# Two heads of each group of four take their second-layer mask as a factor applied by GpSimd, and all rounds run in one piece

## The reference

```
scores = einsum('bhqd,bhkd->bhqk', q, k) / sqrt(DK)
scores = where(mask[:, None, :, :] == 0, NEG, scores)      # NEG = -65504, mask is [16, 256, 1601]
attn = softmax(scores, axis=-1)
out = einsum('bhqk,bhkd->bhqd', attn, v)
```

## Time and profile before

| | |
|---|---|
| median of 3 runs | 5445.89 us (5444.5 to 5447.28) |
| profiled execution | 5421.1 us, of it the span of the core 5419.8 us |
| PE busy | 4887.3 us (90%) |
| DVE busy | 3598.6 us (66%) |
| ACT busy | 2794.9 us (52%) |
| POOL busy | 641.3 us (12%) |
| mean granted PE clock | 0.933 |

### The profile page before, as it was taken

How to read it: one execution, slowest core, us unless ns; L and a number is a source line. 1 busy time by engine, 2 the same in 40 slices (tenths; PEclk the granted TensorE clock), 3 DMA queues, 4 the chain that set the end, 5 groups by cost and what they waited for, 6 DMA issues and landing times.

```text
span 5419.8 us, 103495 instructions
## 1 busy us (share of the span) xinstructions
PE 4887.3 (90%) x41312; PEld 2745.4 (51%) x41312; DVE 3598.6 (66%) x8383; ACT 2794.9 (52%) x5505; POOL 641.3 (12%) x660
## 2 busy tenths in 40 slices
PE   5888888888888888889899999999999999999999
PEld 2455555555555555554455544554455444554456
DVE  4666666666666666566667777777777777777774
ACT  1565565656555556665454444444445444444454
POOL 1111111110111111011110101101010101001000
PEclk7799898989999999897899999999999999999999
DMA  2112222222212222222222222222222222222222
GB/s 60 34 45 52 44 46 52 58 54 50 53 45 43 48 58 54 58 49 70 59 72 69 77 65 70 76 69 65 70 72 69 75 61 78 74 70 64 73 49 65
DMA packets 167992, 327.09 MB, mean 60 GB/s; under 512 B 25656, under 2 KB 76624, under 8 KB 167520
## 3 DMA queue, kind: packets, MB, share of 16 engines
q1 hardware_dynamic: 167520, 320.49, 24.3%
HBM read 237.40 MB, written 4.19 MB: 45 GB/s over the span
## 4 chain that ended last, share of the span: by engine, by line
PE 39%; DVE 8%; SPq 2%; POOL 1%; issue 1%; DMA 1%; ACT 1%; DVEq 0%
PE sums L695 7%; PE a L658 7%; PE d L771 6%; PE a L759 5%; PE a L666 4%; DVE d L811 3%; SPq L1072 2%; PE d L679 1%; PE d L601 1%; PE d L581 1%; PE d L733 1%; PE a L608 1%; PE a L641 1%; DMA kc<-k_hi 1%; PE d L614 1%
## 5 line engine op out<-in xcount | busy, mean ns | idle before, releaser
L967 ACT ACTIVATE probs_c<-a 128x512 f32<-128x512 f32 (+1 forms) x3584 | 1833.9, 563 | 1994.5 <-PE a L666 1992.7
L811 DVE CUSTOM_DVE_ANT_0 d<-d,mcross_q 128x404 f32<-128x404 f32 x2048 | 1138.0, 606 | 341.6 <-PE d L679 337.6
L803 DVE TENSOR_REDUCE chunk_max<-d 128x2 f32<-128x808 f32 x1024 | 1003.2, 998 | 289.0 <-PE d L679 280.5
L695 PE MATMUL sums<-probs_c,vc 128*32 128x256 f32 x13312 | 1119.9, 410 | 13.4 <-PEq L1234 13.2
L666 PE MATMUL a<-qc,kc 25*128 25x256 f32 (+1 forms) x6656 | 931.1, 341 | 129.7 <-ACT probs_c L967 98.5
L666 PEld LDWEIGHTS a<-qc,kc 25*128 25x128 f32 (+1 forms) x6656 | 543.0, 187 | 825.9 <-issue 393.3
L679 PE MATMUL d<-kc,qc 24*128 24x404 f32 x4096 | 912.4, 458 | 47.0 <-DVE chunk_max L811 12.9
L771 PE MATMUL d<-w_back,hidden 128*128 128x128 f32 x4352 | 558.4, 283 | 28.8 <-DVE chunk_max L811 28.8
L759 PE MATMUL a<-xT_e,w_in 128*128 128x256 f32 x2176 | 576.5, 412 | 0.0
L771 PEld LDWEIGHTS d<-w_back,hidden 128*128 128x128 f32 x4352 | 533.5, 197 | 66.8 <-DVE chunk_max L811 39.5
L658 PE MATMUL a<-mcross_k,ident_b 128*128 128x512 bf16 (+1 forms) x1792 | 547.4, 379 | 12.4 <-ACT probs_c L967 12.2
(11 more groups left out here) (157 smaller groups left out, 4441.6 us busy)
## 6 DMA issues: line engine op xcount, KB each, us to landing
w_in<-in_experts SPq DMA_DIRECT2D x272, 256.0 KB, 3.1
w_back<-in_experts SPq DMA_DIRECT2D x272, 256.0 KB, 2.9
kc<-k_hi SPq DMA_DIRECT2D x1024, 50.0 KB
ctxT<-in_ctxT SPq DMA_DIRECT2D x32, 800.5 KB, 5.2
kc<-k_lo SPq DMA_DIRECT2D x512, 50.0 KB
mask_words<-in_mcross SPq DMA_DIRECT2D x32, 800.5 KB
mask_words<-in_mcrossT SPq DMA_DIRECT2D x32, 768.0 KB
out_x<-xe SPq DMA_DIRECT2D x32, 128.0 KB, 1.8
```

What stands on the lines that cost most here:

```text
L695: last = pe.matmul(acc[HP * j:HP * j + HP, :], T["vc"][x.p][0:x.kn, v0:v0 + HP], probs_of(T, x)[0:x.kn, j, half:half + S], start=x.j == 0, ...
L803: done = dve.tensor_reduce(T["chunk_max"][:, x.g % 2, x.i, x.j:x.j + 2, x.c], tile[:].rearrange("p (h n) -> p h n", h=2)[:, :, 0:CHUNK], A ...
L811: done = dve.tensor_tensor_reduce(some, some, mask, 1.0, -3e38, ALU.add, ALU.max, T["chunk_max"][:, x.g % 2, x.i, x.j + h, x.c:x.c + 1])
L967: act.activation(probs_of(T, x)[0:x.kn, x.j, 0:n], tile[0:x.kn, 0:n], ACT.Exp, scale=SCALE).then_inc(M["a_read"], 1)
```

## The change

For heads 0 and 1 of each group (`j < BY_POOL`, the first beat of every kp) layer 1's scores have no mask matmul. After both exponentials are in `probs_c`, POOL cuts them at 2.0 and multiplies them by `factors`, which is `mcross_k / 2^100` (0 or -1) plus `allowed`. `allowed` is 1 where a query has any key left and 2 where it has none. The WV of the even key tile now waits for POOL as well (`multiplied`). Heads 2 and 3 keep the matmul. `factors` is made once for each batch: PE counts each query's masked keys by 13 matmuls of `mcross_k` with ones (MF), DVE turns them into `allowed`, and DVE makes `factors` in five pieces (MB). The self-attention's causal and layer 1 masks share one pair of tiles. The program is one piece, with one `restart`.

```diff
+BY_POOL = 2
+FACTORS = ((0, 3), (3, 6), (6, 9), (9, 12), (12, 13))
...
-        "NC": 0.45, "NS": 0.45, "SV": 0.5}
+        "NC": 0.45, "NS": 0.45, "SV": 0.5, "MF": 1.5, "MB": 0.8}
...
 def cross_masks(self, p, batch):
...
+        out.append(self.put(("found", p), "MF", "mask", p=p))
+        for i in range(len(FACTORS)):
+            out.append(self.put(("factors", p), "MB", p=p, i=i))
+            out[-1].of["found"] = self.at["found", p]
...
 def scores(self, l, p, g, kp, pair):
...
+            if j == BY_POOL - 1:
+                self.at["by_pool"] = sc
...
+                if l and kt % 2 == 0:
+                    step.of["by_pool"] = self.at["by_pool"]
...
+def masked(x):
+    return x.l == 1 and x.j >= BY_POOL
...
-                if y.l:
+                if masked(y):
...
-                                     start=not y.l, stop=not y.l or ends)
+                                     start=not masked(y), stop=not masked(y) or ends)
...
+            if "by_pool" in x.of:
+                pe.wait_ge(M["multiplied"], x.of["by_pool"].c)
...
+        elif x.kind == "MF":
+            pe.wait_ge(M["masks_made"], nth(x.of["mask"]))
+            for kt, (_, kn) in enumerate(spans(SK, P)):
+                last = pe.matmul(tile[:, 0:S], T["ones_b"][0:kn, :], T["mcross_k"][x.p][0:kn, kt, :], start=kt == 0,
+                                 stop=kt == KT - 1)
...
+        elif x.kind == "MF":
+            dve.tensor_scalar(T["allowed"][:], tile[:, 0:S], -BIG * SK, 1.0, ALU.is_equal, ALU.add).then_inc(M["d_read"], 1)
+        elif x.kind == "MB":
...
+            dve.scalar_tensor_tensor(out=T["factors"][x.p][rows, first:last, :], in0=T["mcross_k"][x.p][rows, first:last, :],
+                                     scalar=1.0 / BIG, in1=wide(T["allowed"][rows, :], last - first), op0=ALU.mult,
+                                     op1=ALU.add).then_inc(M["factors_made"], 1)
...
+        elif x.kind == "SC" and x.l == 1 and x.j == BY_POOL - 1:
...
+            pool.wait_ge(M["a_read"], in_ring(x))
+            pool.tensor_scalar(probs, probs, 2.0, 1.0, ALU.min, ALU.mult).then_inc(M["cut_off"], 1)
...
+            pool.wait_ge(M["cut_off"], x.c)
+            pool.tensor_tensor(probs, probs, wide(factors, BY_POOL), ALU.mult).then_inc(M["multiplied"], 1)
...
-    rounds(-1, B - 1)
-    restart()
-    rounds(B, LAST)
+    rounds(-1, LAST)
```

More of the change, by code:

```diff
@@ L308, in scores @@
                 sc.of["mask"] = self.at.get(("mcross", p))
+                sc.of["factors"] = self.at.get(("factors", p))
+            if j == BY_POOL - 1:
+                self.at["by_pool"] = sc
             steps.append(sc)
@@ L441, in numbered @@
     slots = {"d": 2, "a": 3}
-    moved, loaded, groups, tanhs = {}, {}, 0, 0
+    moved, loaded, groups, tanhs, by_pool = {}, {}, 0, 0, 0
     place = {id(x): i for i, x in enumerate(order)}
@@ L461, in numbered @@
             groups += x.last
+        elif x.kind == "SC" and x.l == 1 and x.j == BY_POOL - 1:
+            x.c = by_pool = by_pool + 1
         elif x.kind == "EF" and x.l == 1:
@@ L598, in tensor_program @@
                         pe.wait_ge(M["masks_made"], nth(y.of["mself"]))
-                mask = (T["mself_q"] if y.l else T["causal_q"])[:].rearrange("p a b -> p (a b)")
+                mask = T["mask_q"][:].rearrange("p a b -> p (a b)")
                 for h in range(2):
@@ L606, in tensor_program @@
                     pe.wait_ge(M["d_read"], in_ring(y.of["ns"]))
-                mask = (T["mself_k"] if y.l else T["causal_k"])[:].rearrange("p a b -> p (a b)")
+                mask = T["mask_k"][:].rearrange("p a b -> p (a b)")
                 pe.matmul(T["a"][y.slot][:], T["ident_b"][:], mask, start=True, stop=False)
@@ L751, in tensor_program @@
                                  start=True, stop=True)
+            last.then_inc(M["d_made"], 1)
+        elif x.kind == "MF":
[3 more added lines that the diff above has]
+                                 stop=kt == KT - 1)
             last.then_inc(M["d_made"], 1)
@@ L881, in vector_program @@
             dve.tensor_scalar(dest, view, 0, -BIG, ALU.is_equal, ALU.mult).then_inc(M["masks_made"], 1)
+        elif x.kind == "MF":
+            dve.tensor_scalar(T["allowed"][:], tile[:, 0:S], -BIG * SK, 1.0, ALU.is_equal, ALU.add).then_inc(M["d_read"], 1)
+        elif x.kind == "MB":
+            dve.wait_ge(M["d_read"], in_ring(x.of["found"]))
+            first, last = FACTORS[x.i]
+            rows = slice(0, P if last < KT else SK - first * P)
+            dve.scalar_tensor_tensor(out=T["factors"][x.p][rows, first:last, :], in0=T["mcross_k"][x.p][rows, first:last, :],
+                                     scalar=1.0 / BIG, in1=wide(T["allowed"][rows, :], last - first), op0=ALU.mult,
+                                     op1=ALU.add).then_inc(M["factors_made"], 1)
         elif x.kind in ("RT", "R2", "R3"):
@@ L1011, in pool_program @@
                                ALU.subtract).then_inc(M["q_made"], 1)
+        elif x.kind == "SC" and x.l == 1 and x.j == BY_POOL - 1:
+            n = len(key_tiles(x))
+            probs = probs_of(T, x)[0:x.kn, 0:BY_POOL, 0:n * S]
+            factors = T["factors"][x.p][0:x.kn, 2 * x.i:2 * x.i + n, :].rearrange("p a b -> p (a b)")
+            pool.wait_ge(M["a_read"], in_ring(x))
+            pool.tensor_scalar(probs, probs, 2.0, 1.0, ALU.min, ALU.mult).then_inc(M["cut_off"], 1)
+            if "factors" in x.of:
+                pool.wait_ge(M["factors_made"], nth(x.of["factors"]))
+            pool.wait_ge(M["cut_off"], x.c)
+            pool.tensor_tensor(probs, probs, wide(factors, BY_POOL), ALU.mult).then_inc(M["multiplied"], 1)
         elif x.kind == "RS":
@@ L1105, in mask_tile @@
     if x.i < 2:
-        return (T["mself_q"], T["mself_k"])[x.i][:]
+        return (T["mask_q"], T["mask_k"])[x.i][:]
     if x.i < 4:
@@ L1153, in program @@
         "q_sum": sb("q_sum", [P, NG, S]), "q_high": sb("q_high", [P, NG, S], F32R),
-        "mself_q": sb("mself_q", [P, QT, S], BF16), "mself_k": sb("mself_k", [P, QT, S], BF16),
         "mcross_q": pair("mcross_q", [P, QT, SK], BF16), "mcross_k": pair("mcross_k", [P, KT, S], BF16),
+        "factors": pair("factors", [P, KT, S], BF16), "allowed": sb("allowed", [P, S], BF16),
         "probs_c": pair("probs_c", [P, HG, BANK]), "probs_s": sb("probs_s", [P, HG, BANK]),
@@ L1200, in program @@
     dve.wait_ge(set_up, 16 * (len(loads) + 4))
-    dve.tensor_copy(T["causal_q"][:], T["probs_c"][0][:, 0:QT, 0:S])
-    dve.tensor_copy(T["causal_k"][:], T["probs_c"][1][:, 0:QT, 0:S])
+    dve.tensor_copy(T["mask_q"][:], T["probs_c"][0][:, 0:QT, 0:S])
+    dve.tensor_copy(T["mask_k"][:], T["probs_c"][1][:, 0:QT, 0:S])
     dve.tensor_copy(T["ident_b"][:], T["ident"][:])
+    dve.memset(T["ones_b"][:], 1.0)
     for part in range(3):
```

8 lines of the change are left out of this document (4 added, 4 removed).

## The result

| | before | with the change |
|---|---|---|
| median | 5445.2 us (4 runs) | 5872.6 us (4 runs, 5863.2 to 5879.7) |
| ratio | 1 | 1.0782, 95% interval 1.0767 to 1.0797 |
| profiled execution: span, mean PE clock | 5419.8 us, 0.933 | 5861.9 us, 0.873 |

The account below looks back on a forecast made before the run. PE was taken to bound layer 1 until DVE or POOL is late; 229 masks - 28 MF - 37 POOL - 84 DVE - 20 clock + 18 one piece = 78 us less, timed 5370 us, range 5285 to 5470.

Parts of the forecast that it names:

- DVE's 84: Layer 1, DVE's added work and contention with POOL: 5.2 us a round reaches PE, 84 us lost.
- 37 for POOL with its queues: Layer 1, PE's waits for POOL's new steps and old work queued behind them: 2.3 us a round, 37 us lost.
- 20 for the clock: Layer 1, more PE waits bring a second low-clock stretch in part of the rounds: 20 us lost, between 0 and 56.
- POOL's price: Cut and product on POOL, priced from the split's two steps: 1.12 and 2.36 us, 3.56 us a kp together.
- My upper bound: POOL's cut and product: at most 4.8 us a kp, with a minimum costing as much as a two-input step.
- The first WV of a round: The tightest place in a layer 1 round: PE waits 2.2 us there for POOL's cut and product.
- POOL's product costs more: Rival: product of 3.4 us gives 5460, 4.0 us gives 5570; slower by POOL's price or by DVE, chance 0.18 together.
- This is the ceiling of the main part: Layer 1 mask products of heads 0 and 1 off PE: 3.58 us a group, 229 us gained at most.
- the rival of wider exclusion: Rival: DVE steps reading two SBUF tensors stand still beside POOL: 5430, or 5610; slower by DVE or POOL's price 0.18.
- The barrier: Between the program's two pieces: PE's 13.2 us standstill and the half-speed window after it go, 18 us gained.
- four signs that I had named for being wrong: Product over 3 us, WV waiting for POOL in most kp, DVE over 88% busy, or layer 1 clock below 0.93.

Follow-up runs that it names:

- e7: The kernel before in one piece, with the mask products of heads 0 and 1 of layer 1's cross-attention left out and nothing in their place: 5354.5 us.
- e2: The changed kernel without the cut at 2.0, so POOL only multiplies by the factors: 5560.6 us, ratio 1.0218.
- e6: e2 with every mask product back on PE, so POOL's product is the only difference to e5: 5624.1 us, ratio 1.0334.
- e10: e1 plus POOL fills of a tile nobody reads in each kp (five, three in the last), with the WV waiting for them: 5586.1 us.
- e11: The changed kernel with useless products on PE in seven of the places where it waits for POOL: 5829.7 us, ratio 1.0697.
- e5: The kernel before in one piece, with masked keys counted and factors made but unused, all masks on PE: 5452.3 us, ratio 1.0015.
- e9: e6 with POOL's product replaced by a one-input multiplication by 1.0: 5471.6 us, ratio 1.0043.
- e1: The kernel before with all rounds in one piece, without the second restart; every mask stays on PE: 5429.4 us, ratio 0.9972.

## Why the prediction was wrong

**The ladder.** One piece -16 us (5445 to 5429), factors +23 (5452), the product on POOL +172 (5624), masks of two heads off PE -63 (5561), the cut +312 (5873). My sum had -18, +28 and a share of DVE's 84, 37 for POOL with its queues, -229, and 20 for the clock.

**The step that cost most is POOL's price.** "I take 3.56, since columns and engine are the same": engine and columns were the same, the operation wasn't. The product was well bounded by the earlier trace rows (2.15 against 2.36). The cut I took from a step of multiplications, 1.12 us, and it measured 3.68. My upper bound, "a minimum that costs as much as a two-input step", was below that as well, and the range had its end there. POOL is 5.83 us busy a kp, 24 kp make 140 us, and with the short kp, the splits and the norms it is 169 of a round of 202 us. In my round of 169 that is no longer an engine that "keeps up on average". The first WV of a round waits 2.2 us, as I had put, but by accident: in the round of 3431 us the two steps end 5.9 us after the exponentials and not 3.64, and PE, at 1.2 GHz and held by ACT, comes 3.9 us after them and not 1.5. POOL falls behind later: in most rounds the waits are 2.8, 0.6, 3.9 and 3.9 us in its four groups, where I had 2.2, nothing, nothing and 0.4. The rival "POOL's product costs more" had the mechanism, and its point of decision of 3.3 us a product (with the cut's 1.12 some 4.5 for the pair) was passed by more than 1.3 us. Its price at 4.0, 5570, falls short because it holds no more of the clock than the forecast's 20 us.

**The ceiling was not to be had.** "This is the ceiling of the main part", 229 us: e7 gives 75. The price of the products is right, a beat in which nothing waits is 0.54 us shorter. What failed is the sentence that work taken off PE counts "until DVE or POOL is late": ACT, which my sum never named, is late first, and the clock falls. With 75 us to gain the change would hardly have paid at 3.56 us a kp either: e2 is slower than before with POOL at 2.17.

**DVE and POOL.** "The row shows the lock for a cast only": the rival of wider exclusion was right, and the 5561 us of e2 lie in its 5430 to 5610. The rule that it cited from the Trainium skill (SBUF — State Buffer, Who interferes with whom), on steps with two inputs in SBUF, agrees with the trace. In e6 a piece of the factors, 0.95 us by itself, begins beside the product, as in each of 14 rounds, and is done only 0.8 us after it:

```profile
3300.98 2.13 POOL L1057 TENSOR_TENSOR probs_c<-probs_c,factors 128x1024 f32<-128x1024 f32 x1 [5.82 <-ACT probs_c L1005]
3301.42 2.51 DVE L917 SCALAR_TENSOR_TENSOR factors<-mcross_k,allowed 128x768 bf16<-128x768 bf16 x1
```

Beside fills, which read nothing, the two-input steps run on (e10). But the rival was still too narrow. The router's steps on two columns are held too (171 to 1777 ns), though they have one tensor as input, and fills hold casts. The same section says that casts and tensor_scalar can run in a mode that takes both port pairs, and that such a step and one of GpSimd block each other for a whole instruction. The trace agrees in the 2235 ns of a cast beside a product and the 953 ns beside a fill. It does not agree for the minimum, and there the measurement decides:

```profile
3421.90 3.63 POOL L1055 TENSOR_SCALAR probs_c<-probs_c 128x1024 f32<-128x1024 f32 x1 [1.72 <-ACT probs_c L1005]
3422.06 1.16 DVE L910 TENSOR_SCALAR mask_k<-mask_words 128x512 bf16<-128x512 int32 x1
```

This cast of 0.42 us goes on 0.90 us into the cut, and so do all 13 that begin there; of 16 larger casts that begin 1.2 to 2.4 us into a cut none is held, and of 13 that begin at 3.3 us all are, by 0.17 us. So the cut stops these steps of DVE for about its first 0.9 us and again at its end, not for 3.63. That fits the waits for DVE, 13.5 us a round in the change and 17.3 in e2. Waits for DVE rose by 2.0 us a round for the factors and 6.2 more for the product; I had put 5.2 for both. The maxima weren't held, their mean stayed at 604 ns, as the earlier trace rows let expect.

**The clock is the largest term, and I had sized it from one stretch.** "I put 20 us, between 0 and 56": measured are 20.3 us a round, some 325 for 16 rounds, beside a loss of 427 to the kernel before. I allowed each round one more stretch of 7 us. Down the table the time at 1.2 GHz goes with PE's waits: 8 to 14 us a round with 10 to 13 of waits, 22 to 28 with 16 to 19, 34 with 22, 44 with 27, 59 with 30. e7 has 19.7 with 13.5: there PE has fewer mask products to do as well, and from e6 to e2, where the same products go, the time at 1.2 GHz rises from 22 to 34 while the waits rise by 3.

**What held.** The barrier (18 us, measured 9 to 22), MF (28 us, measured 23 with all of the factors), and the work taken off PE at full clock (11.9 us a round for the masks less MF, where I had 12.5). Of the four signs that I had named for being wrong, only the clock below 0.93 came (0.85). The product is 2.15 us and not over 3, WV waits for POOL in 10 of 28 kp, not in most, and DVE is 66% busy, not over 88%. I had named a sign for the product and none for the cut.

**Still open.** What makes the clock fall for a given pattern of waits; e11 shows only that filling waits raises it. Nor is it settled how much of the product's 172 us is its length and how much its two inputs. A cheaper form of the cut was not found, and the change without it can give wrong results where a masked exponential overflows.

## What to carry to other kernels

An engine's time for one operation says little of another operation of the same size on it, on GpSimd above all: find a row with the same operation, or keep a range that includes three times as much. Before moving work off a PE that is nine tenths busy, make the kernel that merely leaves that work out; here it would have shown a third of the gain in one run. And price each new microsecond of waiting on PE at about two, since the clock went down with it here in e6, e10 and the change; in e5 and e9, with some 2 us a round of waits more than e1, it did not.
